# First x in four pieces with a semaphore each, and the first weight matrix ahead of the small inputs on ScalarE

## The reference

```python
x = L0_attn_x
xn = _layernorm(x, axis=-1)
x = x + _L0_attn_ref(xn, ...) + _L0_ffn_ref(xn, ...)
xn = _layernorm(x, axis=-1)
x = x + _L1_attn_ref(xn, ...) + _L1_ffn_ref(xn, ...)
return x
```

```python
m = jnp.mean(x, axis=axis, keepdims=True)
v = jnp.var(x, axis=axis, keepdims=True)
return (x - m) / jnp.sqrt(v + eps)
```

## Time and profile before

| | |
|---|---|
| median of 3 runs | 432.97 us (432.83 to 433.28) |
| profiled execution, own time | 432.74 us |
| span of its trace | 431.0 us |
| PE busy | 424.1 us, 98% of the span |
| DVE / ACT / POOL busy | 81% / 41% / 39% |
| granted TensorE clock | full in all 40 slices |

### The profile page before, as it was taken

One profiled execution on the slowest core, in us unless ns is written; L12 is line 12 of the kernel. 1 busy time (PEld: TensorE's weight loads), 2 busy tenths in 40 slices (PEclk: granted clock), 3 DMA queues, 4 the chain that ended last, 5 costly groups with the idle time before them and its releaser, 6 DMA issues.

```text
span 431.0 us, 7493 instructions
## 1 busy us (share of the span) xinstructions
PE 424.1 (98%) x2520; PEld 369.8 (86%) x2520; DVE 347.4 (81%) x1090; ACT 177.9 (41%) x333; POOL 166.2 (39%) x198
## 2 busy tenths in 40 slices
PE   7999999999999999999999999999999999999997
PEld 5788889887888898978988989788999889999886
DVE  6787899998899669889996687989979465856785
ACT  5445445424253725441356234322733333525130
POOL 2417379351017200701072905210441054654656
PEclk9999999999999999999999999999999999999999
DMA  8992499970002130000020310000110844521398
GB/s 286 292 420 92 133 295 285 298 192 0 2 10 89 27 121 1 2 2 1 2 79 19 100 50 0 2 1 2 49 51 24 236 156 122 159 102 50 111 229 261
DMA packets 30166, 46.89 MB, mean 109 GB/s; under 512 B 2680, under 2 KB 24464, under 8 KB 29488
## 3 DMA queue, kind: packets, MB, share of 16 engines
q1 hardware_dynamic: 26064, 36.80, 28.3%
q0 software_dynamic: 3072, 8.80, 6.6%
q10 hardware_dynamic: 992, 0.81, 0.6%
HBM read 22.74 MB, written 23.65 MB: 108 GB/s over the span
## 4 chain that ended last, share of the span: by engine, by line
PE 96%; DVE 2%; DMA 1%; ACT 0%; issue 0%; DVEq 0%
PE D L698 28%; PE G L698 25%; PE U L698 25%; PE M L698 10%; PE M L707 1%; PE D L727 1%; PE M L849 1%; PE M L824 1%; DMA rows<-x 1%; PE M L719 1%; PE D L734 0%; PE M L932 0%; DVE w_lo L1355 0%; DVE stats L1365 0%; PE M L918 0%
## 5 line engine op out<-in xcount | busy, mean ns | idle before, releaser
L698 PE MATMUL D<-w_hi,mid_hi 128*128 128x256 f32 x260 | 74.3, 286 | 0.0
L698 PE MATMUL D<-w_hi,mid_lo 128*128 128x256 f32 x260 | 73.6, 283 | 0.0
L698 PE MATMUL D<-w_lo,mid_hi 128*128 128x256 f32 x260 | 73.5, 283 | 0.0
L1103 ACT ACTIVATE mid<-G 128x512 f32<-128x512 f32 x64 | 37.9, 595 | 76.4 <-PE G L698 66.1
L1476 DVE TENSOR_TENSOR mid<-mid,U 128x512 f32<-128x512 f32 x64 | 43.3, 684 | 25.9 <-PE U L698 14.6
L1490 DVE SCALAR_TENSOR_TENSOR rows<-D,weight,rows 128x256 f32<-128x256 f32 x128 | 54.0, 476 | 4.4 <-PE D L698 4.1
L545 POOL TENSOR_TENSOR w_lo<-w_raw,w_hi 128x512 fp32r<-128x512 f32 x35 | 46.9, 1370 | 27.0 <-ACT w_hi L1076 18.6
L1076 ACT ACTIVATE mid_hi<-mid 128x512 fp32r<-128x512 f32 x64 | 39.9, 630 | 37.5 <-DVE mid L1476 37.2
L1355 DVE TENSOR_TENSOR mid_lo<-mid,mid_hi 128x512 fp32r<-128x512 f32 x64 | 48.3, 774 | 6.1 <-ACT mid_hi L1076 4.6
L698 PEld LDWEIGHTS D<-w_hi,mid_hi 128*128 128x128 f32 x260 | 49.8, 191 | 1.7 <-issue 1.0
L698 PEld LDWEIGHTS D<-w_lo,mid_hi 128*128 128x128 f32 x260 | 49.8, 192 | 0.7
(11 more groups left out here) (360 smaller groups left out, 956.4 us busy)
## 6 DMA issues: line engine op xcount, KB each, us to landing
sorted_rows<-weighted SPq DMA_DIRECT2D x8, 1542.0 KB, 18.8
w_raw<-weights SPq DMA_DIRECT2D x5, 1024.0 KB, 18.1
stage<-sorted_rows SPq DMA_DIRECT2D x31, 128.5 KB, 2.3
w_raw<-weights SPq DMA_DIRECT2D x3, 768.0 KB, 11.8
rows<-x SPq DMA_DIRECT2D x7, 256.0 KB, 3.1
part<-rows SPq DMA_DIRECT2D x12, 128.0 KB, 2.0
sums_gate<-part SPq DMA_DIRECT2D x3, 512.0 KB, 6.0
fetched<-returned SPq DMA_DIRECT2D x3, 512.0 KB, 4.8
```

What stands on the lines that cost most here:

```text
L698: ins = nc.tensor.matmul(out_ap, a, b, start=(first and n == 0), stop=(last and n == 3 * len(pairs) - 1))
L1103: nc.scalar.activation(mid[:, c, :], GU[2 * c][:, :], ACT.Silu).then_inc(silu_ready, 1)
```

## The change

The first x is asked for tile by tile: SP issues tiles 0 and 2, ACT tiles 1 and 3, each transfer with its own semaphore `x_tile_loaded[t]`, and `bn_stats` of a tile waits for that tile alone. Waits on `x_loaded` for later groups count one transfer fewer, since group 0 no longer uses that semaphore. Beside that, on ACT `high(0)` moves ahead of the wait for `small_in` and of the three tiny activations.

```diff
+        x_tile_loaded = [sem(f"x_tile_loaded{t}") for t in range(TILES)]
...
+        def load_x_tile(eng, t):
+            eng.dma_start(rows[0][:, t, :], x[t * P:(t + 1) * P, :]).then_inc(x_tile_loaded[t], 16)
...
-            load_x(sp, 0, 0)
+            for t in (0, 2):
+                load_x_tile(sp, t)
             for c in range(6):
                 load_chunk(c)
...
-                    pool.wait_ge(x_loaded[half], at(g, 16, 16))
+                    pool.wait_ge(x_loaded[half], at(g - 1, 16, 16))
...
-            load_x(act, 0, 1)
+            for t in (1, 3):
+                load_x_tile(act, t)
             act.dma_start(small_in[:, :], small[:, :]).then_inc(small_loaded, 16)
...
+            high(0)
             act.wait_ge(small_loaded, 16)
             nc.scalar.activation(shift0[:, 0:1], temp, ACT.Silu).then_inc(table_loaded, 1)
             nc.scalar.activation(lam[:, 0, :], lam[:, 0, :], ACT.Tanh, scale=0.5).then_inc(lam_tanh, 1)
             nc.scalar.activation(decay, decay, ACT.Tanh, scale=0.5).then_inc(decay_tanh, 1)
-            high(0)
             high(1)
             x_norm(0)
...
                 for t in range(TILES):
-                    if t % 2 == 0:
+                    if g == 0:
+                        dve.wait_ge(x_tile_loaded[t], 16)
+                    elif t % 2 == 0:
                         if g < 2:
-                            dve.wait_ge(x_loaded[t // 2], at(g, 16, 16))
+                            dve.wait_ge(x_loaded[t // 2], at(g - 1, 16, 16))
```

## The result

The changed kernel takes 434.02 us (median of 21 runs, 433.25 to 436.05) against 433.08 us before in the same comparison (21 runs, 432.68 to 434.1). The ratio is 1.0023 with a 95% interval of 1.0015 to 1.0031: slower by about 1.0 us. The forecast was +0.4 us with a range up to 434.9. The profiled execution's span is 432.6 us; its own time, 434.32 us at full clock, is 0.3 us above the median, so what its trace shows of the start is probably later than in most executions.

What follows compares the result with a forecast made beforehand. TensorE bounds the kernel (busy 424.1 of 431.0 us), so the change can only move its start. DVE's -0.4 us is covered by ACT and counts 0, ACT adds +0.4, nothing later: 432.97 becomes 433.4 us, range 432.6 to 434.9.

Steps and rivals of the forecast that it cites:

- What sets the start: First 13 us: DVE (7.91) and ACT (7.87) meet at normalisation; DVE gains 0.4 us, ACT loses 0.38; all later moves along.
- The second table load: On ACT between the copy of matrix 0 and the Silu: a load not hidden, 1.28 us plus 0.05 for seams.
- Rival 1: At ACT's table switch: it costs more than the recorded load, by 1.2 us (434.6) up to 435.8; chance 0.20.
- The sum from chunk 0 to the normalisation: On ACT: from chunk 0's landing at 5.49 through copy, load, Silu and matrix 1's copy to normalisation at 8.32.
- The extra transfers: On the issuing queues: chunks and small inputs issued 0.52 us later; chunk 0 lands 0.15 us later, bounds 0 and 0.52.
- Rival 3: Weight chunks land later than by their slot, chunk 0 half a microsecond more: +0.75 to +1.2, 433.7 to 434.2; chance 0.06.
- The clock: TensorE's first real products run slower after longer idling: up to 1.9 us on top, 435.3; chance 0.02.
- the forecast's own case: Whole kernel: +0.2 (chunk 0 not later) to +0.75 us (later by its whole slot), 433.15 to 433.75, centre 433.4; chance 0.64.
- The likeliest case, no measurable change: Whole kernel: time the same within 0.2% (0.87 us); chance 0.71, against 0.27 slower and 0.02 faster.

Runs made afterwards that it cites:

- e8: e3 reordered: ScalarE normalises right behind the copy of matrix 0, VectorE makes matrix 1's low part before x's; 443.30 us, ratio 1.0012, on another chip.
- e2: The kernel before, x still in halves, with only the copy of matrix 0 moved ahead of the small inputs; 433.11 us, ratio 1.0002.
- a1: The changed kernel run again unaltered, for a second trace and time; 433.93 us, ratio 1.0018 to the kernel before.
- e4: The changed kernel with 24 products on zeros instead of 20; 434.12 us, ratio 1.0025 to the kernel before.
- e10: The changed kernel with x in three pieces: tiles 0 and 1 by SyncE, 2 and 3 together by ScalarE; 443.81 us, ratio 1.0016, on another chip.
- e9: e8 with x in two halves as before the change; 444.10 us, ratio 1.0019 to the kernel before, on another chip.
- e5: The changed kernel with tile 2 of x issued by ScalarE, so chunk 0 is in its old slot; 435.22 us, ratio 1.0058 to the kernel before.
- e6: The edits of e3 and e5 together on the changed kernel; 435.19 us, ratio 1.0046 to the kernel before.
- e3: The changed kernel with one table load, by an early Silu on a zeroed column; 432.73 us, ratio 0.9995 to the kernel before.

## Why the prediction was right, and where its size was off

**What sets the start.** Right. DVE and ScalarE met within 0.04 us before, the change put work on ScalarE's side only, and DVE's 0.44 us of gain became 1.66 us of waiting. That all behind the start moves with it one for one holds for the later start (normalisation 1.51 us later, TensorE's product 1.49, span 1.6). It does not hold for the earlier one of e8, where 0.3 of 1.3 us are left at 34 us.

**The second table load.** Right in its place and its price. It costs 1.28 us with seams of 0.01 to 0.02 us (7.32, 7.34, 8.62, 8.63 in the changed kernel; the same in e2). Rival 1, a hidden remainder behind the load, is refuted: the Silu follows at once. The drain of about 1380 ns that the Trainium skill adds to each switch ("ScalarE: Activation LUTs", "What ACT_TABLE_LOAD costs") is not seen in any of the five traces in which work follows such a load at once (the changed kernel, a1, e2, e4, e10); the load itself is, at 1.28 us. The Trainium skill's other page ("ScalarE activation tables: per-element evaluation and per-set limits", "What a function is on this engine") puts two functions of different sets one load of 1283 ns apart, and the traces agree with that.

**The sum from chunk 0 to the normalisation.** Forecast 2.83 us; measured 2.79 (6.66 to 9.45), 2.79 (a1), 2.79 (e4, 6.77 to 9.56) and 2.78 (e10). In e2 it is 2.90, where DVE's shift ends 0.1 us after ScalarE could have begun.

**The extra transfers.** Here the size was off. I bounded the delay of chunk 0 by 0 and 0.52 us and took 0.15, since "the stream is what they wait for, not the request". That was the term that was too small: what stands ahead on the queue mattered. Chunk 0 landed at 5.34, 5.00 and about 5.05 us with x in halves (before, e2, e9). Asked for one slot later it landed at 6.66, 5.72, 6.77 and 6.08 in the four traces with two table loads, and at 5.3 to 6.1 in the five others with that slot: on average 6.0, which is 0.9 us later than the average of the halves, six times the term and beyond its upper bound. With the landing at 6.0 in place of my 5.49 the sum is 0.38 + 0.5 = 0.9 us. The executions at full clock lost 0.6 to 0.7. What drags the landing beyond the slot is not explained. In the nine traces with the later slot the DMA engines moved 210 to 308 GB/s from 3.5 to 4.0 us, in the three with halves 382 to 402. But e5 and e6, with x in pieces and chunk 0 in its old slot, moved 354 and 279, so the rate does not go with the slot alone. Rival 3, to which I gave 0.06, is what happened: half a microsecond more than I took is a landing at 5.99, and its price of 433.7 to 434.2 holds the measured time. The reason that it names, that the pieces each have to be completed first, was not tested by itself.

**The clock.** I gave it 0.02 and at most 1.9 us. It came in a quarter of the executions, which took about 1 us longer than the others (434.4 and above, against 433.7), so it is about 0.25 us of the mean. It is more frequent where TensorE's real work starts later (2 of 54 in the kernel before, 8 of 32 in the changed one, 7 of 11 in e5 and e6), but e4, which starts as late, had 1 of 9. What brings the fall was not isolated.

**Range and chances.** 434.02 lies inside 432.6 to 434.9, and that is in part luck: the forecast's own case ended at 433.75, and the range reached beyond it for rival 1, which did not occur. What filled the room was rival 3 and the clock, to which I had given 0.08 together. The mechanism, a second table load behind a late chunk 0, was right. The likeliest case, no measurable change, had 0.71, and the result falls just beyond its border of 0.2%, at 0.23% with an interval from 0.15 to 0.31.

## What to carry to other kernels

Two edits can each be free and cost a microsecond together: the late chunk was hidden without the second table load, and the table load without the late chunk. Before work is moved ahead of a table function, look at which function now comes first, since a plain copy that comes first brings a table of its own; an early call of the function that needs the right one removes the second load from the path (e3). A transfer that is split on a queue makes everything behind it be asked for later (1.74 instead of 1.34 us here), and a gain on one of two engines that meet is worth no more than the slack of the other.

## What the runs showed of the hardware

In two runs the place of a request on the two queues counted for more than its bytes. In e5 and e6 the first weight chunk was asked for on SyncE's queue at 1.3 us, ahead of the last tiles of x and the small inputs on ScalarE's queue (1.75 and 2.24). The 256 KB chunk landed after 3.4 us in e5 and 3.9 in e6, while a 128 KB tile of x took 5.0 and 6.46 us, and the 23.5 KB of small inputs took 6.5 and 6.8. The tiles that were asked for at 0.8 and 1.3 took 2.3 to 4.1 us in all runs with pieces. Whether it is the later request or the one transfer more ahead on ScalarE's queue was not separated.

The granted TensorE clock can fall in the first 15 us even though the engine, once at work, was never idle for more than 0.9 us at a time (a1, 0.58 in e4 ahead of the transposes). The same transposes with the same gaps left it full in the first trace of the changed kernel, so they are not enough by themselves.
